# State space stage without taps in its projections and as one pipeline of four groups, and stack loads three steps later

## What is computed

```
proj = layernorm(x) @ W_in.T                   # 642 columns
z, xBC, dt_raw = split(proj, 256, 384, 2)
xBC = silu(causal depthwise conv(xBC, 4 taps) + conv_b)
x_ssm (2 heads of 128), B (64), C (64) = split(xBC)
dt = softplus(dt_raw + dt_bias);  A = -exp(A_log)
y[q] = sum over k <= q of (C[q] . B[k]) * exp(cs[q] - cs[k]) * dt[k] * x_ssm[k]     # cs = cumsum(dt * A)
y = (y + x_ssm * D_skip) * silu(z)
x = x + y @ W_out.T
...
```

## Time and profile before

| what | us |
|---|---|
| median of 3 runs | 1668.62 (1665.03 to 1673.44) |
| profiled execution, its own time | 1673.93 |
| its span, first to last instruction | 1671.8 |
| busy in the span: PE, DVE, ACT, POOL | 1253.3, 981.0, 639.5, 573.1 |
| DVE's first statistic of the state space stage | 1173.28 |
| DVE's first statistic of the stage after | 1341.08 |
| mean granted clock of PE | 0.856 |

### The profile page before, as it was taken

One profiled execution on the slowest core, in us unless ns is written; L12 is line 12 of the kernel. 1 busy time (PEld: TensorE's weight loads), 2 busy tenths in 40 slices (PEclk: granted clock), 3 DMA queues, 4 the chain that ended last, 5 costly groups with the idle time before them and its releaser, 6 DMA issues. The chain is left out here.

```text
span 1671.8 us, 30784 instructions
## 1 busy us (share of the span) xinstructions
PE 1253.3 (75%) x9153; PEld 799.4 (48%) x9153; DVE 981.0 (59%) x4171; ACT 639.5 (38%) x1532; POOL 573.1 (34%) x1102
## 2 busy tenths in 40 slices
PE   4799899993482799999945668557778739994786
PEld 2455555542381455555425656456345414543332
DVE  5677777755764777777536635565243338753232
ACT  1356554451131255566522334123232225662221
POOL 3454488872341543544214342243100012210000
PEclk8799999996595699999966977769798958996798
DMA  5435755410112444455001230112000043400000
GB/s 179 140 118 150 219 159 166 148 36 18 44 53 86 141 130 136 149 171 154 27 15 53 66 125 14 35 52 69 15 0 0 0 141 108 124 31 1 0 0 25
DMA packets 139962, 137.80 MB, mean 82 GB/s; under 512 B 12240, under 2 KB 109136, under 8 KB 139552
## 3 DMA queue, kind: packets, MB, share of 16 engines
q1 hardware_dynamic: 131200, 111.40, 21.9%
q0 software_dynamic: 8608, 24.55, 4.6%
HBM read 84.10 MB, written 49.18 MB: 80 GB/s over the span
## 5 line engine op out<-in xcount | busy, mean ns | idle before, releaser
L840 ACT ACTIVATE L0a_Pr<-PS 128x512 f32<-128x512 f32 (+1 forms) x256 | 136.9, 547 | 141.4 <-PE PS L742 89.0
L840 ACT ACTIVATE L1a_Pr<-PS 128x512 f32<-128x512 f32 (+1 forms) x256 | 136.1, 547 | 104.3 <-PE PS L742 51.7
L557 POOL TENSOR_TENSOR L0a_PG<-L0a_Pr,L0a_G 128x512 f32<-128x512 f32 x80 | 105.3, 1320 | 26.6 <-issue 13.0
L963 DVE CUSTOM_DVE_ANT_0 L1a_junk<-PS,L1a_neg 128x256 bf16<-128x256 f32 x256 | 94.8, 420 | 32.1 <-PE PS L715 31.8
L715 PE MATMUL PS<-L0a_Kst,Qm 128*128 128x256 bf16 (+1 forms) x512 | 95.1, 273 | 17.0 <-DVE L0a_mx L963 9.9
L715 PE MATMUL PS<-L1a_Kst,Qm 128*128 128x256 bf16 (+1 forms) x512 | 94.5, 272 | 16.7 <-DVE L1a_mx L963 9.2
L963 DVE CUSTOM_DVE_ANT_0 L1a_junk<-PS,causal_q 128x128 bf16<-128x128 f32 (+1 forms) x256 | 78.5, 353 | 38.1 <-PE PS L715 37.4
L737 PE MATMUL PS<-Qm,L0a_Kst 128*128 128x512 bf16 (+1 forms) x256 | 91.7, 358 | 12.2 <-DMA Qm<-L0a_mT 9.4
L963 DVE CUSTOM_DVE_ANT_0 L0a_junk<-PS,causal_q 128x128 bf16<-128x128 f32 (+1 forms) x256 | 78.5, 352 | 37.1 <-PE PS L715 36.4
L737 PE MATMUL PS<-Qm,L1a_Kst 128*128 128x512 bf16 (+1 forms) x256 | 91.3, 357 | 10.2 <-DMA Qm<-L1a_mT 7.1
L966 DVE TENSOR_REDUCE L3x_mx<-PS 128x2 f32<-128x512 f32 x128 | 84.2, 686 | 23.5 <-PE PS L715 22.9
(11 more groups left out here) (722 smaller groups left out, 3270.8 us busy)
## 6 DMA issues: line engine op xcount, KB each, us to landing
Qm<-q_image SPq DMA_DIRECT2D x160, 128.0 KB
sorted_in<-zeros POOLq DMA_DIRECT2D x16, 516.0 KB, 4.9
L0a_Kst<-k_image SPq DMA_DIRECT2D x64, 128.0 KB
ffn_w_<-L_ffn POOLq DMA_DIRECT2D x32, 256.0 KB, 3.7
L1a_Kst<-k_image SPq DMA_DIRECT2D x64, 128.0 KB
ffn_w_<-L_ffn SPq DMA_DIRECT2D x16, 256.0 KB, 6.9
L3x_Kst<-k_image SPq DMA_DIRECT2D x32, 128.0 KB
k_image<-L0a_kpart SPq DMA_DIRECT2D x16, 192.0 KB
```

Source lines behind the costliest of these rows:

```text
L557: g.tensor_tensor(PG[:, V_ % GATED_RING, :].rearrange("p (h q) -> p h q", h=2), Pr[:, V_ % RING, :].rearrange("p (h q) -> p h q", h=2), G[ ...
L840: a(Pr[:, V_ % RING, 0:2 * nq], PS[:, T_BANK + v % 2, 0:2 * nq], ACT.Exp, scale=SCALE)\
L963: ins = v.tensor_tensor_reduce(junk[:, tt, par, 0:nk], scored[:, par], off, 1.0, LOWEST, ALU.add, ALU.max, mx[:, i % 2, tt, par, hp:hp + 1])
```

## The change

Two edits. In `attention`, STACK_IN goes from (-13, -7) to (-10, -4), so SP issues the first half behind the k parts of the item after and the second behind its q parts. In `state_space`: the weights are packed without spread taps (the stage's small weights go from 2444 to 919 columns); B and C become one projection of 128 columns; the projections are plain; the convolution of each block of 128 channels is one scaled copy and three multiply-adds along the sequence, the x blocks on DVE out of PSUM, the B and C block on POOL from a copy that ACT makes; the loop and its closings go, and four groups run through a table of slots, eight slots apart; softplus and the sums of dt are made for two groups at once, the norm as well, its apply is ACT's; the gating product goes from DVE to POOL; a table of PSUM uses gives PE its waits. The kernel's other arithmetic is as before.

```diff
 # attention
-    STACK_IN, FIRST_STACK_IN = (-13, -7), {"k": -22, "q": -20}
+    STACK_IN, FIRST_STACK_IN = (-10, -4), {"k": -22, "q": -20}
 # state_space
+    PER, R = 8, 2
+    BATCH = ((0, 1), (2, 3))
+    SMALL, XS_BANK, BC_BANK, Z_BANK, LA_BANK = 0, 1, 3, 4, 6
+    TURN = {0: -4, 1: -3, 2: 7, 3: 7}
+    STATS, ROOT, NEWTON, APPLY = (-8, -7), (-7, 1), (-6, 1), {0: -5, 1: -4, 2: 6, 3: 6}
+    RAW, ABS, EXP_DT, ONE, LOG_DT, STEP_DT, SUMS, SUMMED = (1, 8), (1, 8), (1, 9), (1, 9), (1, 9), (2, 10), (3, 11), (3, 12)
+    SPREAD, DECAYS, LOGS, EXPS = (lambda g: 3 if g == 0 else PER * g - 4), (lambda g: 4 if g == 0 else PER * g - 2), \
+        (lambda g: 5 if g == 0 else PER * g), (lambda g: 6 if g == 0 else PER * g + 1)
+    PROJECT, CONV, SILU, TURN_X, TURNED_X, MASK, KERNEL = 0, 1, 2, 5, 6, 6, 7
+    TIMES_X, GATE_IN, GATE, OUT, ADD = 10, 12, 13, 14, 15
+    SLOTS = range(-8, PER * (G - 1) + ADD + 1)
...
+        def conv(v, step, raw, block):
+            out = two(acc[:, block, :])
+            step(v.tensor_scalar(out, raw, tap(block, TAPS - 1), None, ALU.mult))
+            for j in range(1, TAPS):
+                ins = v.scalar_tensor_tensor(out[:, :, j:], raw[:, :, 0:S - j], tap(block, TAPS - 1 - j), out[:, :, j:],
+                                               ALU.mult, ALU.add)
+                if j < TAPS - 1:
+                    step(ins)
...
 # pool
-                with pool.Fori(0, NPASS) as it:
+                for n in SLOTS:
+                    if n == NEWTON[1]:
+                        pool.wait_ge(s["ln_root"], 2)
+                        newton(g_, step, tiles_of(1)).then_inc(s["ln_scale_b"], 1)
+                    g = planned(n, SPREAD)
...
+                    g = group_at(n, CONV + 1)
+                    if g is not None:
+                        pool.wait_ge(s["bc_raw"], g + 1)
...
+                        step.mark(g_.tensor_scalar(out, raw, tap(NH, TAPS - 1), None, ALU.mult))
+                        for j in range(1, TAPS):
+                            step(g_.tensor_scalar(two(part[:, :])[:, :, j:], raw[:, :, 0:S - j], tap(NH, TAPS - 1 - j), None, ALU.mult))
+                            ins = g_.tensor_tensor(out[:, :, j:], out[:, :, j:], two(part[:, :])[:, :, j:], ALU.add)
...
+                            g_.tensor_tensor(y3[:, h, :], y2[:, h, :], zs[:, g % R, h, :], ALU.mult).then_inc(s["y3_ready"], 1)
 # tensor
-                        for k in range(TAPS):
-                            ins = mm(PS[0:64, 2 + n, :].rearrange("p (b t) -> p b t", b=NSEQ), Wbc[:, n, k, :],
-                                     xTp[:, seqs, k:k + S], start=(k == 0), stop=(k == PAD))
+                        mm(PS[:, BC_BANK, :], w("L3a_bc"), xT[:, g, :], start=True, stop=True, **free).then_inc(s["bc_psum"], 1)
-                        for k in range(TAPS):
-                            ins = mm(PS[:, n, :].rearrange("p (b t) -> p b t", b=NSEQ), Wx[:, k, n * P:(n + 1) * P],
-                                     xTp[:, seqs, k:k + S], start=(k == 0), stop=(k == PAD))
+                        mm(PS[:, XS_BANK, :], w("L3a_xs")[:, 0:P], xT[:, g, :], start=True, stop=True, **free).then_inc(s["xs_psum"], 1)
...
 # scalar
+                        a(bcraw[:, :], PS[:, BC_BANK, :], ACT.Copy).then_inc(s["bc_raw"], 1)
...
+                            ins = a(xn[:, t, :], tile(t), ACT.Identity, scale=rstd[:, t:t + 1], bias=shift[:, t:t + 1])
...
+                            a(BC[:, k, :], acc[rows, NH, :], ACT.Silu, bias=w("L3a_bias")[rows, NH:NH + 1]).then_inc(s["bc_ready"], 1)
 # vector
+                            conv(v, step, two(PS[:, XS_BANK + k, :]), k).then_inc(s["xs_conv"], 1)
...
+                        dve.wait_ge(s["dt_one"], k + 1)
+                        step(v.tensor_scalar(dd[:, q, :], w1[:, q, :], 1.0, None, ALU.subtract))
...
```

More of the change, by code:

```diff
@@ L1964, in state_space @@
         sb = core.buffers(c)
[L1965 to L1969, removed]
+        st6, mv = sb("st6", [P, ALL_TILES, 6]), sb("mv", [P, ALL_TILES, 2])
+        var, lnv, r0, nsq, rstd, shift = (sb(n, [P, ALL_TILES]) for n in ("var", "lnv", "r0", "nsq", "rstd", "shift"))
+        xn = sb("xn", [P, ALL_TILES, D])
+        xT = sb("xT", [P, G, NT])
@@ L1983, in state_space, with group_at @@
-        y2 = sb("y2", [P, NH, NT])
-        y3 = sb("y3", [P, NH, NT])
+        y2, y3 = sb("y2", [P, NH, NT]), sb("y3", [P, NH, NT])
         tri2 = core.W[:, COLS["tri"][0]:COLS["tri"][0] + S]
-        core.n_setup += 4
+        tile = lambda t: core.X[:, t, :]
+        two = lambda ap: ap.rearrange("p (b t) -> p b t", b=NSEQ)
+        tiles_of = lambda k: slice(T * BATCH[k][0], T * (BATCH[k][-1] + 1))
+        tap = lambda block, k: w("L3a_taps")[:, block * TAPS + k:block * TAPS + k + 1]
+        def group_at(n, off):
+            g, r = divmod(n - off, PER)
+            return g if r == 0 and 0 <= g < G else None
@@ new lines, in listed, with planned @@
+        def listed(n, table):
+            return [k for k in range(len(table)) if table[k] == n]
+        def planned(n, slot_of):
+            return next((g for g in range(G) if slot_of(g) == n), None)
+        def conv(v, step, raw, block):
[6 more added lines that the diff above has]
+                    step(ins)
+            return ins
@@ new lines, in newton @@
+        def newton(ops, step, q):
+            step(ops.tensor_tensor(nsq[:, q], r0[:, q], r0[:, q], ALU.mult))
+            step(ops.tensor_tensor(nsq[:, q], nsq[:, q], var[:, q], ALU.mult))
+            step(ops.tensor_scalar(nsq[:, q], nsq[:, q], -0.5, 1.5, ALU.mult, ALU.add))
+            step(ops.tensor_tensor(rstd[:, q], r0[:, q], nsq[:, q], ALU.mult))
+            step(ops.tensor_tensor(shift[:, q], mv[:, q, 0], rstd[:, q], ALU.mult))
+            return ops.tensor_scalar(shift[:, q], shift[:, q], -1.0, None, ALU.mult)
@@ L1998, in _ @@
             def _(pool):
[L1999 to L2007, removed]
@@ L2089, in _ @@
                 a = nc.scalar.activation
-                act.wait_ge(s["setup"], core.n_setup)
                 step = Step(act, s["act_step"])
-                act_layernorm(core, act, step, L)
-                for g in range(ALL_TILES // 4):
-                    act.wait_ge(s["xT_psum"], g + 1)
-                    a(xTp[:, g * NSEQ:(g + 1) * NSEQ, PAD:PAD + S], PS[:, g, :].rearrange("p (b t) -> p b t", b=NSEQ),
-                      ACT.Copy).then_inc(s["xT_ready"], 1)
-                end_pass(core, act, "go_act")
```

477 lines of the change are left out of this document (310 added, 167 removed).

## The result

The changed kernel takes **1643.2 us** (median of 4 runs, 1642.0 to 1646.4) where the kernel before, run beside it, takes 1669.7: a ratio of **0.9845, interval 0.9821 to 0.9870**, 26.5 us less. The forecast was 1611, and 1643 lies above its range. The profiled execution took 1643.95 us with a span of 1642.1, against 1673.9 and 1671.8.

A forecast was written before the change was run, and what follows sets the result against it. PE was taken as the bound while it projects, with everything waiting for everything afterwards. State space -53 and stacks -5 gave -58 against 1673.9, 1615.9 profiled; against 1668.6 that is 1611 us, range 1596 to 1638.

The forecast's parts named there:

- I take 0.64, the row whose operations are alike: State space stage, POOL's third-block convolution: each multiply priced at 0.64 us, the block at 7.0 us, other end 12.2.
- B: Rival: POOL's convolution sets the state space period if its multiply costs 1.94 us; +14 us, 1625; chance 0.12.
- the lock: State space step sizes: DVE steps with two SBUF inputs may wait out POOL additions, up to 7.6 us once; counted as nothing.
- C: Rival: DVE and POOL lock each other out in the state space step sizes; +8 us, 1619; chance 0.08.
- ACT's nine table loads: nothing: State space stage: ACT's table loads stand beside DVE's convolutions and cost nothing while DVE and PE set the period.
- the attention stages within 10 us: Sign of error: the prediction is wrong if the attention stages change by more than 10 us either way.
- The walk and its corrections: New state space stage in program order: 102.7 us, plus 8 for a 0.85 clock and 4 for hand-overs: 115 instead of 168.
- Rival D: PE's clock falls to the head's 0.60 for the whole state space stage; +23 us, 1634; chance 0.10.
- The stacks: Attention: stacks fetched three steps later cut PE's waits for row maxima; -5 us, bounds 0 and -16.5; 3 us in hand.
- Rival F: Slower: later stacks miss their slot in attention, through late loads or SP held by q parts; 1680; chance 0.04.
- E: Rival: the stacks were what held up the maxima in attention; all 16.5 us come back, 1600; chance 0.04.
- A: The forecast itself, whole kernel: 1611 us, own range 1600 to 1622; chance 0.62.

## Why the prediction was wrong

By profiled executions the sum was -58 and the result is -30.0.

**"I take 0.64, the row whose operations are alike", and the chance of 0.12 for B.** This is the first step that failed. The multiply costs 1.57 us. It stands between my two ends, but what follows from it is rival B: the block ends behind the step sizes instead of with them, and groups 2 and 3 wait for it. The run with additions alone prices the block at 13.0 us together with the stretch of the step sizes: 10.1 in the two groups, as B had them, and 2.9 ahead of them, which are the stretch and not B's spread copy. I chose between 0.64 and 1.94 by the kind of operation, and left aside that both rows differ in the types they read and write. The timeline of before has one float32 row of this operation wider than four columns, which I did not look for:

```profile
5.51 0.39 POOL L514 TENSOR_SCALAR L0a_den<-W 128x64 f32<-128x64 f32 x1 [0.97 <-DMA W<-small_common]
```

Four columns take 0.20 there (L1604). By the slope between the two, an estimate from one instruction, 512 columns take 1.8 us; they took 1.57. With it the block is 11.6 us and B's waits belong in the sum.

**"I leave it at nothing in the sum", the lock.** The reason given, that the steps end with POOL's convolution in any case, held only for a block of 7.0 us. With one of 10.4 the steps run wholly beside it: 2.2 us longer in the first batch and 1.6 in the second (4.4 and 3.8 against 2.2), within C's 8. The rule of the Trainium skill (SBUF — State Buffer, Who interferes with whom) agrees with what is seen beside POOL's additions: single steps of 0.17 us last 1.26, as long as one addition. It does not beside the multiplies, which read SBUF too: of the steps that run there, one lasts 0.54 and the others 0.17 to 0.25. I had counted the six steps with two inputs in SBUF, but L2332, which waits longest, is a tensor_scalar with one; the same section counts tensor_scalar among the operations that can take the shared ports. The lock is inside the 13.0, not beside it; by that rule alone the stage would have been 123.

**"ACT's nine table loads: nothing", and the attention stages within 10 us.** Inside the stage the term was not seen to cost; where ACT also had the scaled copies, two loads lay in its late chain. What was missing is a term outside it. I counted the loads of the stage and never asked which set it leaves behind and who relies on it. That is 16.7 us in the cross attention, and one line takes 15.2 of them back. No rival had it, so this is the larger fault.

**The walk and its corrections.** With the POOL block short the stage took 117.3 against 115. The end of the last kernel, 92.5 in the walk and 104.5 with its two corrections (8 for the clock, 4 for hand-overs), is at 105.5 in that run. Right in sum, but not in place, and that the sum came out is in part luck: the corrections spread a clock of 0.85 over the stage, that run has 0.79, and 10.7 of these us are there before the third group's first convolution (72.9 against 62.2), in the head and the second batch, where PE works at half its rate behind each wait; the sums alone take 5.1 instead of 2.6. The full period is 17.8 for 16.6. Rival D was nearer than I had it: the stage's clock is 0.76, but its 0.60 never held for a whole stage. Most of what is left is the closing, 3.70 for 2.42, which clears 18 semaphores more (36 of the stage's own where it had 18). Other closings in the trace of before go the same way, 3.1 to 3.6 us with 33 of a stage's own and 4.85 with 56, but no run changed the number alone: that it is the reason was only argued.

**The stacks.** -5 against -9.0 alone (5.5 to 12.5) and -7.5 at the end: within its bounds, sized low. Rival F's mechanism exists, one shift further on: at (-10, -4) there is no wait for a stack beyond each stage's first items, at (-7, -1) the kernel is 36 us slower. In L1 that is SP held behind the mask, which F named for the q parts. So that the stack had time in hand is shown, that it was 3 us is not.

**E and A.** Maxima all back: no, 11.3 us of 16.5 stay even so. A's stage took 15 us more than its 115, of which 13.0 are POOL's block with the lock, 1.3 the closing, 1.0 the walk.

## What to carry to other kernels

When a stage is rewritten, write down the state it leaves, not only its time: which table set ACT holds, and which later stage took that for granted; one load by name at the end costs 1.3 us of an idle engine and was worth 20. Price an operation by a row with the same operation, types and memories, even if it is much smaller, and where there is none give the dear end the larger chance if a queue stands behind it. In a pipeline whose chain goes round all engines a block is best put where its engine waits anyway, even if that engine does more work for it.

## What the runs showed of the hardware

A POOL multiply by a scalar over 128x512 float32 in SBUF takes 1.49 us with a constant and 1.57 with a per-partition operand, while an addition of two such tensors took 1.26 in the changed kernel. Where additions follow one another in a block, their place counts: with the parts made by ACT the first of three took 1.27 and the others 1.08, and in the run with additions alone 1.04 (one tensor as both inputs), 1.27 and 1.08. Why is open.

A table load was 1.283 us in every row, and the next activation started 0.02 us behind its end (1359.11 + 1.28, then 1360.41).

A DVE step of 128x16 beside such an addition lasts until the addition ends (1.26 to 1.28 us instead of 0.17), in the changed kernel and with POOL working for nobody. Beside the multiply one step lasts 0.54 to 0.55 and the rest, but for a last one of 0.43, are not longer, also where both inputs are in SBUF.

At the low clock (0.50 granted in both stretches) an instruction of two columns and one of sixteen cost PE the same: four of two columns are followed by the next group 0.87 us later (1187.89 to 1188.76), two of sixteen 0.45 later (1184.90 to 1185.35), 0.22 each.

Filling PE's waits with products raised the granted clock of the stage from 0.76 to 0.89 and, in the head, from 0.56 to 0.85, and gained 2.5 to 3.7 us of the stage. Where 4.98 us without work lay between the added products and the sums, the sums ran at 0.54, nearly all at the low level (1.2 GHz).
